# Layer 1's row maxima over whole rows, columns scaled ahead, and layer 3's V parts side by side

## The chip, the cores and the metric

The kernel runs on one core of one Trainium2 chip. The metric is the device time of one execution in microseconds. Its matrix engine is called TensorE (PE in the profile, PEld for its weight loads), and besides it there are VectorE (DVE), ScalarE (ACT), GpSimd (POOL), and SyncE (SP), which here only issues DMAs.

## The reference, cut to what matters

Eight graphs of 1024 nodes with 128 features go through four attention layers that share one adjacency matrix. Each layer's output is added to its input and normalised. Layer 0 and 1 are dot product attention with four heads of 32, layer 2 is additive with one head of 128, layer 3 additive with four heads of 32:

```python
# layer 1
scores = jnp.einsum('bhnd,bhmd->bhnm', q, k) / jnp.sqrt(jnp.float32(HD))
scores = jnp.where(adj[None, None] == 0, -jnp.inf, scores)
attn = jnp.nan_to_num(jax.nn.softmax(scores, axis=-1), nan=0.0)
# layers 2 and 3
e = ei[:, :, :, None] + ej[:, :, None, :]
e = jnp.where(e > 0, e, ALPHA * e)
e = jnp.where(adj[None, None] > 0, e, MASK_VAL)
att = jax.nn.softmax(e, axis=-1)
h = jnp.einsum('bhij,bhjd->bhid', att, Wh)
```

## The kernel before, in words

The program is a row of stages: `node(0)`, `heads(0)`, `node(1)`, `heads(1)` and so on to `node(4)`. A node stage goes over the eight graphs, makes the projections and stores them in DRAM. A heads stage runs one attention layer over its *units*, a unit being one head of one graph: 32 units in layers 0, 1 and 3, eight in layer 2. Four units make the body of a loop (`UNROLL`).

A unit has 16 *tiles* of 128 keys by 512 queries, eight for the first half of the queries and eight for the second. TensorE makes the scores of a tile in a PSUM bank, ScalarE takes the exponential, which is kept in a high part `phi` and, made by a subtraction (`take_low`, line 334), a low part `plo`; GpSimd makes the low part, VectorE every fourth in layer 1. Six tiles later (`LAGS`) TensorE weighs V with both parts (`weigh`). V is in three bf16 parts of 33 columns (32 and a column of ones for the sum): the high part of the weight meets all three, the low part two. In layer 1 a product takes the three parts side by side, 99 and 66 columns (lines 1095, 1097), into three results that VectorE adds. In layer 3 there are five products of 33 columns (line 1113), all into one result, and three more for rows without neighbours (line 1120).

PSUM has eight banks. In layers 1 to 3 the scores go round four of them (`RING`), banks 4 and 5 hold scores for the maxima, 6 and 7 the sums. The softmax needs each row's maximum, the *shift*, before the unit's first tile. In layer 1 `top_scores` multiplies 128 queries by 512 keys, with the maximum taken by `take_max` (line 1399) over each half row, 16 of them a unit, in a rhythm of one for each tile, one and a half units ahead. `find_shift` joins the halves (line 1362), `turn_shift` has TensorE transpose the result (line 1033), `shift_rows` copies it from PSUM (line 1377), and SP writes it in one transfer into row 96 of `qs` (`place_shift`, line 534). In layers 2 and 3 `spread` fills banks 4 and 5 with one row for all partitions (line 1010), `take_max` takes eight maxima of 1024 columns (line 1389), and `find_shift` makes the shift (lines 1367, 1368) and three scaled columns `colx` (1369 to 1371). The shift is placed by eight transfers of 128 elements (line 530). `settle` (line 1432) and a relu on ScalarE (line 839) prepare the argument of the exponential in layers 2 and 3. Lines 1070 and 1072 are the products of scores there, 1056 and 1057 in layer 1.

Each maximum waits for the one before:

```python
dve.wait_ge(s_nmax, CREDIT + TILES * U + k)
it, c = k // 2, k % 2
dve.wait_ge(s_nsc, TILES * U + k + 1)
```

At the end of each half unit `half_done` (lines 1479 to 1486) divides the sums by the last column and puts them in `outp`. SP's queue runs in this order in a unit: store the previous unit, place the next unit's shift, load the unit three ahead. Line 1325 copies the columns of a graph in stages 2 and 3 out of PSUM; `turn_x` on TensorE (line 935) waits for it. Line 1458 is layer 0's reduction over eight key blocks. In layer 1 a unit's loads are needed when its first `top_scores` comes up.

Of the kernel before, what the change touches and what calls it, by code (L numbers as in the profile page):

```python
# [34 lines left out]
P = 128  # L35
# [23 lines left out]
SHIFT_CREDIT = 1  # L59
# [5 lines left out]
MAX_AT = 8  # L65
TURN_AT = 11
TURN_BANK = 5

SPREAD_AT = 7
MAX_NEXT = {1: 6, 2: 7}  # L70
FIND_AT = 4
MAX_AFTER = {7: 0, 9: 1, 11: 2, 13: 3, 14: 4, 15: 5}
# [6 lines left out]
LOADS = (9, 7, 7, 8)  # L79
ROWMS = (0, 1, 8, 8)  # L80

SKEW = (0, 2, 2, 2, 1)
HCHAIN = (36, 32, 52, 28)
HLEFT = (7, 4, 6, 3)
# [6 lines left out]
def build(nc, t):  # L91
    with ExitStack() as ctx:
# [18 lines left out]
        col_d = nc.dram_tensor("col_d", (GRAPHS * 8, P, BLOCKS), F32, kind="Internal").ap()  # L111
# [46 lines left out]
        colp = sb("colp", [P, 8, BLOCKS])  # L158
# [17 lines left out]
        cols = sb("cols", [P, UNROLL, 2, BLOCKS])  # L176
        colx = sb("colx", [P, UNROLL, 3, BLOCKS])
# [11 lines left out]
        junk = full[:, 1, :].bitcast(BF16)[:, 0:NODES]  # L189
# [4 lines left out]
        shrow = sb("shrow", [BLOCKS, 2, P], F32R)  # L194
# [3 lines left out]
        sums = work[:, 0:2, :].rearrange("p t f -> p (t f)")[:, 0:IB * 33].rearrange("p (t d) -> p t d", d=33)  # L198
# [26 lines left out]
        s_colx = sem("s_colx")  # L225
# [14 lines left out]
        s_shT = sem("s_shT")  # L240
        s_shift = sem("s_shift")
# [108 lines left out]
        def max_count(U):  # L350

            return CREDIT + TILES * SHIFT0[2] + BLOCKS * (U - SHIFT0[2])
# [36 lines left out]
        def _(sp):  # L389
# [31 lines left out]
            def node(stage):  # L421
# [17 lines left out]
                def store_parts(b):  # L439
# [7 lines left out]
                    else:  # L447
                        n = 2 * HEADS[stage]
                        sp.wait_ge(s_ev["row2"], ev("row2", stage, b))
                        for kind in range(4):  # L450
# [3 lines left out]
                        sp.dma_start(col_d[bass.ds(b * 8, n)].rearrange("r p t -> p r t"), colp[:, 0:n, :]  # L454
                                     ).then_inc(s_pst[q], 16)
# [35 lines left out]
            def load_unit(layer, u, m):  # L491
# [16 lines left out]
                else:  # L508
# [7 lines left out]
                    for k in range(2):  # L516
                        go(cols[:, n, k, :], one(col_d, r + k * heads).rearrange("a p t -> (a p) t"))
# [7 lines left out]
            def place_shift(layer, g, n):  # L525
                if layer > 1:

                    sp.wait_ge(s_shcol, SHIFT0[layer] + g + 1)
                    for it in range(BLOCKS):
                        sp.dma_start(qs[96:97, n, it * P:(it + 1) * P].bitcast(F32), nshift[:, n % 2, it:it + 1]  # L530
                                     ).then_inc(s_rowm[n], 16)
                    return
                sp.wait_ge(s_shift, SHIFT_CREDIT + SHIFT0[layer] + g + 1)
# [54 lines left out]
        def _(pool):  # L588
# [110 lines left out]
            node(0)  # L699
            heads(0)  # L700

            pool.memset(ks[96:97, :, :].bitcast(F32), 1.0).then_inc(s_krow, 1)
            pool.wait_ge(s_krow, 1)
            node(1)
            heads(1)
# [903 lines left out]
```

## Time and profile before

| what | value |
|---|---|
| median of 3 runs | 3119.71 us (3115.49 to 3122.32) |
| profiled execution | 3143.97 us, its span 3142.2 us |
| busy, share of span | PE 77%, PEld 53%, DVE 70%, ACT 50%, POOL 58% |
| layer 0, about | 150 to 760 us |
| layer 1, about | 950 to 1685 us |
| layer 2, about | 1885 to 2205 us |
| layer 3, about | 2370 to 3065 us |
| mean granted clock of TensorE | 0.837 |

The rest of the span is node stages. Times in the trace count from the start of the span. A row of the timeline gives start and duration of one instruction, and in brackets how long its engine had been idle and what released it. A busy time is the time in which an engine had an instruction at work; a TensorE instruction in the trace lasts longer than its share, since matmuls overlap, so distances between starts say more.

### The profile page before, as it was taken

Reading aid. Unit: us, or ns where it says so; the run is one execution under the profiler, and the core shown is the slowest. Engines: PE = TensorE matmul, PEld = TensorE weight load, DVE = VectorE, ACT = ScalarE, POOL = GpSimd, SP = SyncE. Lnnn points to the kernel's source line nnn. Section 1 sums busy time; section 2 is a strip of 40 time slices with the busy share of each in tenths; the row PEclk is TensorE's granted clock in tenths of the full one; section 3 lists DMA queues with packets and bytes.
Section 4 is the critical chain, followed back from the end, with each engine's and each line's share of the span. In section 5 each row is a group of like instructions: output and inputs, shape, how many; then the busy total and the mean of one; then the engine's idle time right before and its main releaser. Section 6 shows DMA issues by size and latency. Waiting matters only on the chain.

```text
span 3142.2 us, 90847 instructions
## 1 busy us (share of the span) xinstructions
PE 2413.1 (77%) x33112; PEld 1668.6 (53%) x33112; DVE 2194.8 (70%) x4654; ACT 1585.7 (50%) x2273; POOL 1829.2 (58%) x1837
## 2 busy tenths in 40 slices
PE   5588888885657888888885758888466999999990
PEld 3366666664533555555554535667343666666660
DVE  4499999997656777777774335443456988888874
ACT  2344444453652444444443533444463777777775
POOL 2388888886433555555564433344323877777782
PEclk8788888887777999999997767889676988888995
DMA  7922222232653121212113641110452111111117
GB/s 236 300 73 74 73 73 73 73 74 47 192 206 85 49 54 45 56 45 52 48 46 80 185 146 42 49 32 15 132 133 56 49 48 49 39 47 49 44 25 162
DMA packets 299864, 263.65 MB, mean 84 GB/s; under 512 B 193080, under 2 KB 257080, under 8 KB 299504
## 3 DMA queue, kind: packets, MB, share of 16 engines
q1 hardware_dynamic: 294896, 241.82, 28.4%
q0 software_dynamic: 4608, 16.78, 1.5%
q8 instruction: 257, 4.21, 0.6%
q14 instruction: 103, 0.84, 0.1%
HBM read 162.84 MB, written 95.36 MB: 82 GB/s over the span
## 4 chain that ended last, share of the span: by engine, by line
PE 38%; issue 22%; DVE 22%; ACT 7%; POOL 3%; DMA 2%; DVEq 1%; SPq 1%; ACTq 0%; POOLq 0%
PE ps L1113 13%; PE ps L1072 4%; DVE xn L1458 4%; DVE full L1399 4%; PE ps L1010 3%; DVE full L1389 2%; PE ps L948 2%; PE ps L1053 2%; ACT xn L728 2%; PE ps L1065 2%; DVE cv L1420 2%; PE ps L1070 2%; POOL xc L334 2%; PE ps L1024 2%; PE ps L972 2%
## 5 line engine op out<-in xcount | busy, mean ns | idle before, releaser
L334 POOL TENSOR_TENSOR xc<-part 128x512 f16<-128x512 f32 x1536 | 1579.6, 1054 | 824.2 <-ACT part L865 672.5
L1113 PE MATMUL ps<-vs,part 128*128 128x33 bf16 (+1 forms) x13824 | 854.2, 189 | 45.8 <-DVEq L1490 44.5
L1113 PEld LDWEIGHTS ps<-vs,part 128*128 128x128 bf16 x13824 | 680.0, 101 | 362.3 <-issue 206.6
L1113 PE MATMUL ps<-vs,xc 128*128 128x33 bf16 (+1 forms) x9216 | 781.0, 187 | 3.8 <-issue 3.8
L1113 PEld LDWEIGHTS ps<-vs,xc 128*128 128x128 f16 x9216 | 597.5, 99 | 0.0
L865 ACT ACTIVATE part<-ps 128x512 f32<-128x512 f32 x512 | 305.8, 597 | 434.3 <-PE ps L1057 434.1
L1399 DVE CUSTOM_DVE_ANT_0 full<-ps,mask_n 128x512 bf16<-128x512 f32 x512 | 353.0, 690 | 161.9 <-DVE top L1399 61.0
L1389 DVE CUSTOM_DVE_ANT_0 full<-ps,mask_n 128x1024 bf16<-128x1024 f32 x320 | 390.4, 1220 | 108.0 <-PE ps L1010 79.4
L847 ACT ACTIVATE part<-cv,lift 128x1024 f32<-128x1024 f32 x256 | 294.8, 1152 | 322.0 <-DVE cv L1420 297.0
L1072 PE MATMUL ps<-qs,sel 128*128 128x512 f32 x640 | 420.1, 658 | 0.0
L1053 PE MATMUL ps<-qs,ks 128*128 128x512 f32 x512 | 290.6, 570 | 120.3 <-DVE cv L1420 88.2
L1432 DVE SCALAR_TENSOR_TENSOR cv<-ks,colx,ps 128x512 f32<-128x512 f32 x320 | 238.7, 746 | 186.5 <-PE ps L1072 145.9
L865 ACT ACTIVATE part<-cv,cols 128x512 f32<-128x512 f32 x320 | 229.9, 718 | 265.3 <-DVE cv L1432 249.4
L1024 PE MATMUL ps<-ks,qs 96*128 96x512 f32 x512 | 253.6, 506 | 116.6 <-DVE top L1399 94.2
L1420 DVE SCALAR_TENSOR_TENSOR cv<-ps,mask_t 128x1024 f32<-128x1024 f32 x256 | 311.8, 1219 | 44.5 <-PE ps L1053 22.0
L1057 PE MATMUL ps<-qs,ks 97*128 97x512 f32 x512 | 307.1, 600 | 0.0
L865 ACT ACTIVATE part<-ps,colx 128x512 f32<-128x512 f32 x320 | 215.1, 672 | 69.6 <-PE ps L1072 65.4
L1095 PE MATMUL ps<-vs,part 128*128 128x99 bf16 x2048 | 232.7, 213 | 1.8 <-POOL xc L334 1.8
L1095 PEld LDWEIGHTS ps<-vs,part 128*128 128x128 bf16 x2048 | 164.2, 99 | 129.8 <-issue 103.9
L839 ACT ACTIVATE ps<-ks,colx 128x512 f32<-128x512 f32 x316 | 218.7, 692 | 11.5
L1097 PE MATMUL ps<-vs,xc 128*128 128x66 bf16 x2048 | 219.3, 195 | 0.0
L1056 PE MATMUL ps<-mask_t,ident_b 128*128 128x512 bf16 x512 | 205.0, 400 | 0.4
(151 smaller groups left out, 3607.5 us busy)
## 6 DMA issues: line engine op xcount, KB each, us to landing
qs<-q_d SPq DMA_DIRECT2D x224, 128.0 KB
ks<-k_d SPq DMA_DIRECT2D x224, 128.0 KB
ks<-row_d SPq DMA_DIRECT2D x40, 512.0 KB
vs<-v_d SPq DMA_DIRECT2D x96, 198.0 KB
q_d<-part SPq DMA_DIRECT2D x32, 512.0 KB
k_d<-part SPq DMA_DIRECT2D x32, 512.0 KB
ctx_d<-xn SPq DMA_DIRECT2D x96, 128.0 KB, 1.7
xc<-ctx_d SPq DMA_DIRECT2D x96, 128.0 KB, 4.6
```

What stands on the lines that cost most here:

```text
L334: eng.tensor_tensor(plo[:, r, :], prob[:, r, :], phi[:, r, :], ALU.subtract).then_inc(low_done(layer, u, s)[0], 1)
L847: act.activation(prob[:, r:r + 2, :], arg[:, a:a + 2, :], ACT.Exp, scale=2.0 * CLIP, bias=lift[:, 0:1]).then_inc(s_exp, 2)
L865: act.activation(prob[:, r, :], src, ACT.Exp, **more).then_inc(s_exp, 1)
L1024: pe.matmul(bank, qs[0:96, n, it * P:(it + 1) * P], ks[0:96, n, cut], start=True, stop=True).then_inc(s_nsc, 1)
L1053: mm = pe.matmul(bank, ks[:, n, blk_j], qs[:, n, cut], start=True, stop=True)
L1057: mm = pe.matmul(bank, ks[0:97, n, blk_j], qs[0:97, n, cut], start=False, stop=True)
L1072: mm = pe.matmul(bank, sel[:, 2, :], qs[:, n, cut], start=False, stop=True, skip_group_check=True)
L1095: pe.matmul(ps[:, 6 + c, at_a:at_a + V3], phi[:, r, it * P:(it + 1) * P], vs[:, n, at_v:at_v + V3], start=opens, stop=False, skip_group_ch ...
L1113: mm = pe.matmul(acc, half[:, r, it * P:(it + 1) * P], vs[:, n, at:at + width], start=opens and h == 0 and v == 0, stop=h == 1 and v == 1, ...
L1389: dve.tensor_tensor_reduce(junk[:, :], pf[:, 4 * HALF:6 * HALF], mask_n[:, k, :], 1.0, LOWEST, ALU.add, ALU.max, accum_out=top[:, k, 0:1]) ...
L1399: dve.tensor_tensor_reduce(junk[:, 0:HALF], ps[:, 4 + c, :], mask_n[:, it, c * HALF:(c + 1) * HALF], 1.0, LOWEST, ALU.add, ALU.max, accum_ ...
L1420: dve.scalar_tensor_tensor(arg[:, a:a + 2, :], ps[:, r:r + 2, :], -0.5, mask_t[:, j:j + 2, c * HALF:(c + 1) * HALF], ALU.max, ALU.min).the ...
```

## The change

**Layer 1's maxima.** `top_scores` makes two products into a pair of banks, (2, 3) or (4, 5) in turn, and `take_max` takes the maximum of the whole row of 1024 straight into `nshift`: eight a unit. A maximum waits for the last but one. The scores' ring in layer 1 becomes two banks, 0 and 1. `turn_shift`, `shift_rows` and layer 1's `find_shift` go; the shift is placed by eight transfers as in layers 2 and 3, and row 96 of `ks` holds -1 where it held 1. The maxima of the unit after next come at tiles 5, 7, 9, 11, 13 and 15, the last two at tiles 1 and 3 of the next.

**Scaled columns.** `colx` goes. The node stages 2 and 3 make five columns for each head (two copies, three scalings), one DMA loads them.

**Layer 3.** The products are layer 1's (99 and 66 columns), and the correction is one product of 99. `half_done` in layers 1 and 3 takes the divisor from the first part, scales all three parts into `sums` (384 elements), and a reduction adds them into `outp`.

In all three layers the maxima write their unused output to two buffers in turn (`junks`).

```diff
-MAX_AT = 8
-TURN_AT = 11
-TURN_BANK = 5
+MAX_NEXT = ({}, {1: 6, 3: 7}, {1: 6, 2: 7}, {1: 6, 2: 7})
+MAX_AFTER = ({}, {5: 0, 7: 1, 9: 2, 11: 3, 13: 4, 15: 5}) + ({7: 0, 9: 1, 11: 2, 13: 3, 14: 4, 15: 5},) * 2
...
-LOADS = (9, 7, 7, 8)
-ROWMS = (0, 1, 8, 8)
+LOADS = (9, 7, 6, 7)
+ROWMS = (0, 8, 8, 8)
...
-        junk = full[:, 1, :].bitcast(BF16)[:, 0:NODES]
+        junks = [full[:, k, :].bitcast(BF16)[:, 0:NODES] for k in range(2)]
...
-                    for k in range(2):
-                        go(cols[:, n, k, :], one(col_d, r + k * heads).rearrange("a p t -> (a p) t"))
+                    go(cols[:, n, :, :], one(col_d, g).rearrange("a p k t -> (a p) k t"))
...
+                if layer == 1:
+                    sp.wait_ge(s_nmax, max_count(g + 1))
+                else:
+                    sp.wait_ge(s_shcol, SHIFT0[layer] - SHIFT0[2] + g + 1)
+                for it in range(BLOCKS):
+                    sp.dma_start(qs[96:97, n, it * P:(it + 1) * P].bitcast(F32), nshift[:, n % 2, it:it + 1]
+                                 ).then_inc(s_rowm[n], 16)
...
@@ top_scores
+                    at = 2 + 2 * (k % 2)
+                    pe.wait_ge(s_nmax, max_count(U) + k - 1)
+                    for c in range(2):
+                        mm = pe.matmul(ps[:, at + c, :], qs[0:96, n, k * P:(k + 1) * P],
+                                       ks[0:96, n, c * HALF:(c + 1) * HALF], start=True, stop=True)
+                    mm.then_inc(s_nsc, 1)
...
-                            bank = ps[:, s % RING, :]
+                            bank = ps[:, s % (2 if layer else RING), :]
...
-                                pe.wait_ge(s_exp, T - RING + 1)
+                                pe.wait_ge(s_exp, T - 2 + 1)
...
-                            if layer == 1:
+                            if layer in (1, 3):
...
+                                if layer == 3 and j == BLOCKS - 1:
+                                    at_i = c * HALF + it * P
+                                    mm = pe.matmul(ps[:, 6 + c, at_a:at_a + V3], empty[:, at_i:at_i + P], zs[:, n, :],
+                                                   start=False, stop=True, skip_group_check=True)
...
-                        dve.tensor_copy(colp[:, 0:n, :], ps[:, 4, 0:BLOCKS * n].rearrange("p (t r) -> p r t", r=n)
-                                        ).then_inc(s_ev["col"], 1)
+                        for k in range(2):
+                            dve.tensor_copy(colp[:, 0:heads, k, :], got[:, :, k, :])
+                        dve.tensor_scalar(colp[:, 0:heads, 2, :], got[:, :, 1, :], SLOPE - 1.0, None, ALU.mult)
+                        dve.tensor_scalar(colp[:, 0:heads, 3, :], got[:, :, 1, :], 1.0 - SLOPE, None, ALU.mult)
+                        dve.tensor_scalar(colp[:, 0:heads, 4, :], got[:, :, 1, :], SLOPE, None, ALU.mult
+                                          ).then_inc(s_ev["col"], 1)
...
@@ take_max
+                    dve.wait_ge(s_nmax, max_count(U) + k - 1)
+                    if layer == 1:
+                        src, least, dst = pf[:, (2 + 2 * (k % 2)) * HALF:][:, 0:NODES], LEAST, nshift[:, n % 2, k:k + 1]
+                        dve.wait_ge(s_nsc, BLOCKS * U + k + 1)
...
+                    dve.tensor_tensor_reduce(junks[k % 2], src, mask_n[:, k, :], 1.0, least, ALU.add, ALU.max,
+                                             accum_out=dst).then_inc(s_nmax, 1)
...
@@ half_done
-                            if layer == 1:
-                                acc = sums
-                                link(dve.tensor_reduce(acc, ps[:, bank, 0:IB * V3].rearrange(
-                                    "p (t v d) -> p t d v", v=3, d=33), AX.X, ALU.add))
...
+                            link(dve.tensor_scalar(rden[:, 0:blocks], acc[:, :, 0, width], TINY, None, ALU.max))
                             link(dve.reciprocal(rden[:, 0:blocks], rden[:, 0:blocks]))
...
+                            link(dve.tensor_tensor(sums, acc[:, :, :, 0:width],
+                                                   scale.unsqueeze(3).to_broadcast([P, blocks, parts, width]), ALU.mult))
+                            link(dve.tensor_reduce(o, sums.rearrange("p t v d -> p t d v"), AX.X, ALU.add))
```


## Rows read from the trace of the kernel before

**Rows 1.** Windows, three attention layers: us, each engine's busy us, granted clock, DMA share.

```profile
1000.00:1640.00 640.00, 545.22 (x5021) 331.41 (x5020) 481.32 (x1303) 271.14 (x454) 366.97 (x341) 0.97 0.20 50
1960.00:2160.00 200.00, 169.09 (x1787) 132.37 (x1785) 90.30 (x201) 84.77 (x122) 82.43 (x81) 0.85 0.12 35
2440.00:3040.00 600.00, 563.50 (x10953) 383.95 (x10951) 521.87 (x1002) 450.33 (x691) 465.35 (x461) 0.90 0.18 44
```

**Rows 2.** Waits in layer 1, 1000 to 1640: total us, times, longest.

```profile
PE ps L1024 <- DVE top L1399: 90.7, 107, 2.4
DVE full L1399 <- DVE top L1399: 52.3, 196, 0.3
```

**Rows 3.** Groups by line, VectorE in layer 1: busy us, mean ns, idle before.

```profile
L1399 DVE CUSTOM_DVE_ANT_0 full<-ps,mask_n 128x512 bf16<-128x512 f32 x453 | 312.3, 689 | 133.5 <-DVE top L1399 52.3 <-PE ps L1024 34.4 <-DVE xn L1486 30.5
L334 DVE TENSOR_TENSOR xc<-part 128x512 f16<-128x512 f32 x113 | 85.2, 754 | 4.9 <-PE ps L1097 4.4 <-DVE nshift L1362 0.4
...
L1479 DVE TENSOR_REDUCE work<-ps 128x132 f32<-128x396 f32 x57 | 32.2, 566 | 0.0
```

**Rows 4.** Layer 1's shift by line: ns min/median/max, first and last start.

```profile
L1362 DVE SCALAR_TENSOR_TENSOR nshift<-top x32: 166/167/462, 969.0 to 1661.7; 128x8 f32<-128x8 f32 x32
```

**Rows 5.** Timeline, TensorE's score products near layer 1's end: start, us.

```profile
1655.51 0.59 PE L1057 MATMUL ps<-qs,ks 97*128 97x512 f32 x1
...
1656.61 0.59 PE L1057 MATMUL ps<-qs,ks 97*128 97x512 f32 x1
...
1659.57 0.59 PE L1057 MATMUL ps<-qs,ks 97*128 97x512 f32 x1
...
1660.35 0.58 PE L1057 MATMUL ps<-qs,ks 97*128 97x512 f32 x1
```

**Rows 6.** Layer 3's shift by line, 2440 to 3040.

```profile
L1368 DVE SCALAR_TENSOR_TENSOR nshift<-shift x29: 166/966/966, 2446.2 to 3031.7; 128x8 f32<-128x8 f32 x29
```

**Rows 7.** Timeline, VectorE in layer 3: end of a half, maxima, a settle.

```profile
2603.97 0.16 DVE L1483 TENSOR_SCALAR rden<-ps 128x4 f32<-128x4 f32 x1
...
2604.38 0.29 DVE L1486 TENSOR_TENSOR xn<-ps,rden 128x128 f32<-128x128 f32 x1
2605.05 1.22 DVE L1389 CUSTOM_DVE_ANT_0 full<-ps,mask_n 128x1024 bf16<-128x1024 f32 x1 [0.38 <-DVE xn L1486]
...
2606.20 0.74 DVE L1432 SCALAR_TENSOR_TENSOR cv<-ks,colx,ps 128x512 f32<-128x512 f32 x1
2606.86 1.22 DVE L1389 CUSTOM_DVE_ANT_0 full<-ps,mask_n 128x1024 bf16<-128x1024 f32 x1
```

**Rows 8.** Timeline, TensorE's score products in layer 3.

```profile
2471.33 0.58 PE L1072 MATMUL ps<-qs,sel 128*128 128x512 f32 x1
...
2472.30 0.58 PE L1072 MATMUL ps<-qs,sel 128*128 128x512 f32 x1
```

**Rows 9.** Layer 0's reduction in SBUF by line.

```profile
L1458 DVE TENSOR_REDUCE xn<-work x64: 1898/1998/2025, 161.1 to 746.9; 128x128 f32<-128x1024 f32 x64
```

**Rows 10.** Timeline, opening of layer 3: SP's small transfers and their release.

```profile
2387.01 22.65 SPq L530 DMA_DIRECT2D qs<-nshift  x16
...
2393.53 0.58 PE L1070 MATMUL ps<-mask_t,ident_b 128*128 128x512 bf16 x1 [2.09 <-DMA qs<-nshift]
```

**Rows 11.** Timeline, TensorE at a turn of layer 3's loop.

```profile
2647.51 0.60 PE L1070 MATMUL ps<-mask_t,ident_b 128*128 128x512 bf16 x1 [3.69 <-issue]
```

**Rows 12.** Windows behind a turn of layer 1's loop.

```profile
1150.00:1158.00 8.00, 5.85 (x34) 3.50 (x34) 4.08 (x12) 1.55 (x4) 2.08 (x2) 0.57 0.00 1
1158.00:1162.00 4.00, 4.00 (x39) 2.35 (x38) 3.50 (x8) 2.25 (x4) 3.13 (x3) 1.00 0.00 0
```

**Rows 13.** Timeline, VectorE in layer 3: first scaled column, next settle.

```profile
2611.84 0.15 DVE L1369 SCALAR_TENSOR_TENSOR colx<-cols 128x8 f32<-128x8 f32 x1
...
2613.13 0.75 DVE L1432 SCALAR_TENSOR_TENSOR cv<-ks,colx,ps 128x512 f32<-128x512 f32 x1
```

**Rows 14.** The copy of the columns: who waited for it (us, times).

```profile
  PE ps L935: 40.7, 14
```

More of the change, by code:

```diff
@@ L525, in place_shift @@
             def place_shift(layer, g, n):
[L526 to L533, printed above, removed]
-                sp.dma_start(qs[96:97, n, :].bitcast(F32).rearrange("a (t p) -> a t p", p=P),
-                             shrow[:, n % 2, :].bitcast(F32)).then_inc(s_rowm[n], 16)
+                if layer == 1:
[5 more added lines that the diff above has]
+                                 ).then_inc(s_rowm[n], 16)
             def store_output(layer, g, n):
@@ L852, in exps @@
                         if layer == 1:
-                            src, more = ps[:, r % RING, :], dict(scale=SCALE)
+                            src, more = ps[:, s % 2, :], dict(scale=SCALE)
                             act.wait_ge(s_score, T - CREDIT + 1)
@@ L1115, in weigh @@
                                                    skip_group_check=True)
-                            if layer == 3 and j == BLOCKS - 1:
-                                at_i = c * HALF + it * P
-                                for v in range(3):
-                                    mm = pe.matmul(acc, empty[:, at_i:at_i + P], zs[:, n, v * 33:(v + 1) * 33],
-                                                   start=False, stop=v == 2, skip_group_check=True)
                         mm.then_inc(s_av, 1)
@@ L1150, in heads @@
+                            if tt in MAX_AFTER[1] and one_after:
+                                if MAX_AFTER[1][tt] == 0:
+                                    unit_ready((n + 2) % UNROLL, u + (n + 2) // UNROLL)
+                                top_scores((n + 2) % UNROLL, MAX_AFTER[1][tt], U + 2)
                 if layer:
                     U = SHIFT0[layer]
-                    if layer == 1:
-                        unit_ready(0, 0)
-                        for k in range(TILES):
-                            top_scores(0, k, U)
-                        turn_shift(0, U)
-                    else:
-                        for n in range(2):
-                            unit_ready(n, 0)
-                            spread(n, U + n)
@@ L1162, in heads @@
-                    if layer == 1:
-                        unit_ready(1, 0)
-                        pe.wait_ge(s_shift, SHIFT_CREDIT + U + 1)
-                        for k in range(TILES - MAX_AT):
-                            top_scores(1, k, U + 1)
+                    for n in range(2):
+                        unit_ready(n, 0)
+                        if layer > 1:
+                            spread(n, U + n)
+                            continue
+                        for k in range(BLOCKS if n == 0 else len(MAX_AFTER[1])):
+                            top_scores(n, k, U + n)
@@ L1229, in _ @@
             dve.memset(bias3[:, :, :], 0.0).then_inc(s_fill, 1)
-            left, cut = work[:, 0:4, :], junk[:, 0:HALF].rearrange("p (k f) -> p k f", f=F)
+            left, cut = work[:, 0:4, :], junks[1][:, 0:HALF].rearrange("p (k f) -> p k f", f=F)
             given = rows[:, 0:4, :]
@@ L1405, in body @@
+                    if k == BLOCKS - 1 and layer > 1:
+                        dve.wait_ge(s_nmax, max_count(U + 1))
                 def body(u, first, last):
```

161 lines of the change are left out of this document (47 added, 114 removed).

## The prediction

> **What bounds the kernel now.** I read the windows of the three attention layers that change [rows 1]. No engine is full in layer 1: TensorE has work in 545 of 640 us, VectorE in 481. So I asked the waits who is late [rows 2]: TensorE stands 90.7 us at the score products for the maxima, behind VectorE's previous maximum, and VectorE itself stands 52.3 us behind its own accumulator. The groups of VectorE [rows 3] give the size: a maximum over 512 columns takes 0.69 us and has 0.29 us of idle time before it, 0.98 us in all, 16 times a unit, 15.7 us. The shift is found once a unit, 32 times from 969.0 to 1661.7 [rows 4]: 692.7 us over 31 periods, 22.35 us a unit. TensorE's own need is read where it is not held up [rows 5]: successive score products are 1.10 us apart with one product for a maximum in between (1655.51 to 1656.61) and 0.78 us without (1659.57 to 1660.35). Sixteen tiles need 17.6 us. So layer 1 goes at VectorE's pace and has 4.75 us a unit to lose.
>
> Layer 3 is another case. Its period is (3031.7 - 2446.2) / 28 = 20.91 us [rows 6]. VectorE works in 521.9 of 600 us [rows 1]; its slots are tight [rows 7]: a maximum over 1024 columns 1.15 us from start to start, a settle 0.66 us, one after the other, eight of each 14.5 us. TensorE's tiles are 0.97 us apart [rows 8], 15.5 us for sixteen, and two one-row products come on top. Both engines are close to the bound. Layer 2 has VectorE at 90 of 200 us: what the change does there on VectorE lies in its idle time.
>
> **Layer 1, step by step.** The maxima become eight of 1024 columns. They no longer wait for their predecessor (two junk buffers), so each is 1.15 to 1.22 us: 9.5 us instead of 15.7. Four subtractions at 0.75 us stay [rows 3], 3.0 us. The end of a half unit changes: in layer 3 it now lasts 1.08 us, 2603.97 to 2605.05, with a product of 128 elements of 0.29 us [rows 7]. After the change the product covers 384 elements: the 396 elements of the old layer 1 reduction took 0.57 us [rows 3], so 0.55, +0.26. Behind it comes a new reduction of 384 elements in SBUF. Bounds: 0.57 us by the reduction from PSUM; from above by layer 0's reduction, 1024 elements, 1.998 us [rows 9], which also jumps between the terms of each sum: less a fixed 0.15 it is 1.8 ns an element, so 0.84 us. I take the upper, the nearer in memory and pattern; with a gap the half grows by 1.15 us to 2.25, two of them 4.5 us. VectorE then needs 9.5 + 3.0 + 4.5 = 17.0 us, TensorE still 17.6 (same products, one transpose less): TensorE becomes the bound, by little. The transpose and VectorE's copy of its result go and free VectorE.
>
> *The shift's way.* It was one transfer after tile 11. Now eight small ones wait for the eighth maximum (tile 3), but on SP's queue they stand behind the store of the previous unit, which waits for the end of its half, about tile 6. I reckon: tiles 0 to 5 of the unit 6.0 us (six at 0.78 and four products for maxima at 0.32), tile 5's own two products to 6.7, their maximum to 7.9, the end of the half to 10.0, the store 0.5 (an allowance), then eight transfers. In the opening of layer 3 they take from 2387.01 to the release at 2393.53, 6.5 us [rows 10]. That lands at 17.0 us, and the next unit starts at 17.6. So it is hidden by 0.6 us alone; if VectorE runs late by more, all of it shows. The seven loads stand behind these issues and end early enough for the maxima of two units on (needed at tile 5 of the next unit), again with little over. I put 0.3 us on the unit: 17.9.
>
> *The scores' ring* falls from four banks to two. A bank must be read before it is written again: scores, then the exponential. Two tiles last 1.56 us even without products for maxima, 2.2 us with. The exponential runs beside them. I cost it at nothing; without its cover it is a rival below.
>
> *The turn of the loop.* TensorE stands still for 3.69 us at the start of a body [rows 11], and the clock then falls: in 1150 to 1158 the granted clock is 0.57, so mostly the lower level of 1.2 GHz, and 34 matmuls start, where the next 4 us at 1.00 (2.4 GHz) start 39 [rows 12]. Eight microseconds did the work of 3.5, 4.5 lost with an idle of 2.15; with an idle of 3.7 it is 6.1, per unit 1.5. While VectorE set the pace this was partly hidden; with TensorE as bound it counts: 17.9 + 1.5 = 19.4, rounded to 19.5. **Layer 1: 31 x (22.35 - 19.5) = 88 us less.** Bounds: 17.9 (no turn cost) is 138 less; 20.6 (VectorE late by 1.1 us) is 54 less. The opening has 16 maxima at about 0.95 before any score, then 8 at 1.2: 5 us less.
>
> **Layer 3.** Twenty matmuls of 33 columns in each tile become eight of 99 and 66. The nearest rows are the tiles themselves: 0.97 us here, 0.78 us in layer 1 with just such a tile [rows 5, 8], so TensorE gets 16 x 0.19 = 3.0 us a unit, and 16 of 24 correction products. VectorE loses 2 x 1.15 = 2.3 us at the halves. It wins the three scaled columns: from 2611.84 to the settle at 2613.13, 1.29 us [rows 13], of which 0.2 comes back as a wait: 1.1. Adjacent maxima win 0.2. Its idle time is 78 us in some 29 units, 2.7 us each; I let TensorE's relief take 0.5 of it. Net +0.5 us a unit, **16 us more**. Bounds: a reduction of 0.57 and 1.0 us of waits gone, -0.5 a unit, 16 less; nothing gone, +1.0, 32 more.
>
> **The rest.** In stages 2 and 3 one copy of the columns becomes five small operations, and TensorE waits for this copy, 40.7 us over 14 times [rows 14]. A small operation takes 166 ns at least [rows 6], and these overlap since none waits for another; I take 0.1 us for each of the four added, bounds 0 and 0.166: 16 x 0.4 = 6 us more, at most 11. The column loads are one DMA fewer a unit, hidden in SP's idle time; stored pieces are longer. The openings of layers 2 and 3 lose some 14 waits behind an accumulator, 4 us less. Layer 2's steady part: 0.
>
> **Sum:** -88 - 5 + 16 + 6 - 4 = -75. The profiled execution took 3143.97 us, span 3142.2, 0.8% over the median of 3119.71. 3144 - 75 = 3069; on the median 3045 us.
>
> **Rivals.**
> *A, more is won:* layer 1 runs at TensorE's 17.6 with the turn cheaper, or layer 3, freed of TensorE, gains: 120 to 150 us less, 2985. For it: cold stretches also hit layer 3's TensorE, clock 0.90 [rows 1]. Against: VectorE's tight slots [rows 7].
> *B, less is won:* the shift's 0.6 us of cover is gone, or VectorE sets 20.6 us: 54 and 5 won, 32 and 6 lost, 4 won: 25 less, 3095.
> *C, slower:* the new reduction in SBUF waits for GpSimd. A small operation on SBUF there, nshift, is 166 ns when GpSimd is idle and 966 at the median beside it [rows 6]. If reduction and product each wait 0.8 us, 3.2 us a unit in both layers: VectorE needs 20.2 in layer 1, with the turn 21.7, a gain of 20; layer 3 loses 32 x 3.7 = 118. With the rest that is 95 more, 3215. It is slower from about 1.6 us a unit on (75 = 31 x (1.6 - 0.9) + 32 x 1.6). Against: layer 0's reduction spans 1898 to 2025 ns with GpSimd busy [rows 9], no such scatter. The Trainium skill (GPSIMD Engine Reference, the row on SBUF interfaces in section 1) names DVE instructions with two SBUF inputs or in a 2-port mode as those that contend; the product has one SBUF input, the reduction one, nshift two, which agrees with the spread above.
> *D, the clock:* with two banks TensorE idles briefly and often and drops to 1.2 GHz. Layer 1 before had 90.7 us of such stops at 0.97 [rows 1, 2], so against. If a quarter of layer 1 were cold, its unit would be 17.6 x 1.25 = 22, with the turn 23.5: 36 more there, and 13 for the rest: 3170. The Trainium skill warns of it (TensorE: Matmul & The Clock Gate, "A second HAM failure mode: psum-queue depth-cycling"): cycling through PSUM banks makes the clock oscillate. No row here shows it without a longer stop.
>
> **Numbers.** Forecast case (3015 to 3075) 0.47, A 0.22, B 0.18, C 0.07, D or no gain at all 0.06. Two in ten left out: 2985 to 3095. This kernel's measurement tells 0.2% (6 us). Faster 0.87, same 0.03, slower 0.10.
>
> **What the new profile would show.** Layer 1: TensorE's waits for maxima gone, period near 19.5, VectorE's reduction at 0.84 us, the release of tile 0 by the DMA of nshift rare. Layer 3: period 21.4, VectorE over 0.9 busy, TensorE's tiles with gaps, and its clock no lower. Wrong if tile 0 waits for nshift each unit, if the reduction is over 1.2 us, or if layer 1's clock falls below 0.9.

## The result, and the profile after

The changed kernel takes 2980.9 us (median of 4 executions, 2975.7 to 2990.5) where the kernel before takes 3121.0: a ratio of 0.955, 95% interval 0.952 to 0.958. The forecast was 3045 us, the range 2985 to 3095. The direction was right, the gain of 140 us almost twice the 75 forecast. The profiled execution is the longest of the four, 2990.5 us, its span 2988.8.

The windows of the changed kernel, as [rows 1] (layers 1, 2 and 3):

```profile
1000.00:1500.00 500.00, 487.81 (x4984) 302.40 (x5076) 462.42 (x806) 275.59 (x463) 397.77 (x346) 1.00 0.28 64
1800.00:2000.00 200.00, 167.38 (x1899) 135.33 (x1929) 90.83 (x192) 90.54 (x130) 88.07 (x86) 0.91 0.12 35
2260.00:2860.00 600.00, 504.28 (x4611) 300.08 (x4692) 514.55 (x933) 425.38 (x658) 440.07 (x439) 0.84 0.16 42
```

TensorE is busy 98% in layer 1 (85% before) at full clock, while layer 3's clock fell from 0.90 to 0.84. The waits in layer 1, as [rows 2]:

```profile
DVE full L1344 <- DVE xn L1436: 28.3, 57, 0.6
...
PE ps L1034 <- DMA qs<-nshift: 7.9, 17, 1.6
PE ps L1034 <- issue: 2.2, 3, 1.0
DVE full L1344 <- PE ps L1009: 1.9, 4, 0.9
```

TensorE's 90.7 us behind maxima are gone and nothing of that size came instead; the shift's transfers cost 7.9 us in 500. They were not rare, as forecast: tile 0 waited for them 17 times in some 29 units. VectorE's groups there, as [rows 3]:

```profile
L1344 DVE CUSTOM_DVE_ANT_0 full<-ps,mask_n 128x1024 bf16<-128x1024 f32 x229 | 274.7, 1215 | 31.2 <-DVE xn L1436 28.3 <-PE ps L1009 1.9 <-issue 1.0
L328 DVE TENSOR_TENSOR xc<-part 128x512 f16<-128x512 f32 x116 | 123.1, 1061 | 0.3 <-DVE xn L1436 0.3
L1436 DVE TENSOR_REDUCE xn<-work 128x128 f32<-128x384 f32 x58 | 34.6, 596 | 2.0
L1434 DVE TENSOR_TENSOR work<-ps,rden 128x384 f32<-128x384 f32 x58 | 32.3, 557 | 2.0
```

The new reduction takes 0.60 us, the low part rose from 0.75 to 1.06. A layer's length is read here from its first to its last exponential. First the kernel before, then the changed one (duration, first and last start; the first row is layer 1, the second spans layers 2 and 3):

```profile
L865 ACT ACTIVATE part<-ps x512: 597/597/603, 978.0 to 1678.0; 128x512 f32<-128x512 f32 x171
L865 ACT ACTIVATE part<-cv,cols x320: 705/722/728, 1900.4 to 3058.3; 128x512 f32<-128x512 f32 x160
```

```profile
L855 ACT ACTIVATE part<-ps x512: 591/597/599, 970.6 to 1522.1; 128x512 f32<-128x512 f32 x171
L855 ACT ACTIVATE part<-cv,cols x320: 704/721/727, 1740.9 to 2902.4; 128x512 f32<-128x512 f32 x160
```

Read so for every run (us from the first to the last exponential of a layer, one profiled execution each; "median" is of the whole kernel):

| kernel | layer 1 | layer 2 | layer 3 | median, executions |
|---|---|---|---|---|
| before | 700.0 | 304.2 | 659.2 | 3121.0, 4 |
| before, once more (`y1`) | 699.7 | 283.3 | 658.8 | 3123.1, 1 |
| changed | 551.5 | 284.2 | 683.8 | 2980.9, 4 |
| `x1` parts in PSUM | 550.8 | 283.6 | 668.6 | 2972.4, 4 |
| `x2` columns by VectorE | 551.1 | 284.2 | 681.5 | 2996.7, 4 |
| `x3` one junk buffer | 553.9 | 283.9 | 666.3 | 2988.1, 4 |
| `x5` layer 1's part alone | 548.5 | 304.0 | 668.5 | 2985.8, 4 |
| `x4` before, short maxima | 635.8 | 283.7 | 658.6 | 3055.5, 1 |
| `y2` more instructions | 593.0 | 284.3 | 658.7 | 3007.5, 1 |
| `y4` more low parts | 602.1 | 284.3 | 680.4 | 3031.2, 1 |
| `z1`, `z2`, `z4` padded | 554.9, 551.8, 552.6 | 294.0, 304.1, 283.5 | 670.9, 708.8, 679.4 | 2989.5, 3030.8, 2977.5, 1 each |
| `z3` before, padded | 698.4 | 283.9 | 658.5 | 3115.5, 1 |
| `x7` spread early | 551.8 | 284.0 | 750.1 | 3051.5, 4 |
| `x8` spread early, parts in PSUM | 550.9 | 283.8 | 680.9 | 2982.9, 4 |
| `x9` spread early, layer 1's part alone | 550.8 | 284.8 | 681.8 | 2990.7, 1 |
| `y3` filler | 552.2 | 284.3 | 651.3 | 2952.4, 4 |
| `z5` filler, layer 2's spread early | 552.4 | 283.7 | 657.9 | 2958.4, 4 |
| `z6` half filler | 552.0 | 283.6 | 661.1 | 2966.1, 4 |

The ledger from `y1` (3123.1 us) to the changed kernel's profiled execution (2990.5): the start of layer 1 -7.6, layer 1 -148.2, the stage behind it with layer 2's opening -5.0, layer 2 +0.9, the next stage -0.5, layer 3 +25.0, the rest +2.8. Sum -132.6.

### The profile page after: what moved, and what is told of

Its sections match the earlier page's. It is cut to its first block, busy times and chain, and to the rows that moved or that the text cites. A ratio compares the mean times of both kernels' runs of the same rounds, so it can differ in the third digit from the quotient of the medians.

```text
span 2988.8 us, 75947 instructions
## 1 busy us (share of the span) xinstructions
PE 2279.6 (76%) x26182; PEld 1544.6 (52%) x26424; DVE 2185.2 (73%) x4086; ACT 1581.0 (53%) x2273; POOL 1846.1 (62%) x1837
## 4 chain that ended last, share of the span: by engine, by line
PE 37%; DVE 22%; issue 19%; ACT 7%; SPq 5%; DMA 4%; POOL 2%; DVEq 1%; ACTq 0%; POOLq 0%
PE ps L1092 8%; PE ps L1050 4%; DVE xn L1402 4%; DVE full L1344 4%; PE ps L1000 3%; SPq L526 3%; PE ps L1073 3%; PE ps L1031 3%; PE ps L938 2%; DVE cv L1364 2%; DVE cv L1376 2%; ACT xn L720 2%; PE ps L1009 2%; PE ps L1075 2%; PE ps L1035 2%
## 5 line engine op out<-in xcount | busy, mean ns | idle before, releaser
L1344 DVE CUSTOM_DVE_ANT_0 full<-ps,mask_n 128x1024 bf16<-128x1024 f32 x576 | 695.2, 1218 | 173.8 <-PE ps L1000 106.2
L1092 PE MATMUL ps<-vs,part 128*128 128x33 bf16 (+1 forms) x7680 | 504.5, 193 | 45.8 <-DVEq L1437 44.5
L1073 PE MATMUL ps<-vs,part 128*128 128x99 bf16 x4096 | 496.4, 218 | 2.8 <-POOL xc L328 2.8
L1075 PE MATMUL ps<-vs,xc 128*128 128x66 bf16 x4096 | 468.9, 200 | 0.0
L1092 PE MATMUL ps<-vs,xc 128*128 128x33 bf16 (+1 forms) x5120 | 458.7, 191 | 3.5 <-issue 3.5
L1050 PE MATMUL ps<-qs,sel 128*128 128x512 f32 x640 | 424.2, 664 | 26.7 <-DVE cv L1376 21.2
L1075 PEld LDWEIGHTS ps<-vs,xc 128*128 128x128 f16 x4096 | 360.9, 103 | 0.0
L1376 DVE SCALAR_TENSOR_TENSOR cv<-ks,cols,ps 128x512 f32<-128x512 f32 x320 | 238.4, 745 | 156.5 <-PE ps L1050 130.0
L1364 DVE SCALAR_TENSOR_TENSOR cv<-ps,mask_t 128x1024 f32<-128x1024 f32 x256 | 311.8, 1219 | 42.9 <-PE ps L1031 19.3
L1092 PEld LDWEIGHTS ps<-vs,xc 128*128 128x128 f16 x5120 | 342.0, 100 | 0.0
L855 ACT ACTIVATE part<-ps,cols 128x512 f32<-128x512 f32 x320 | 214.8, 671 | 74.3 <-PE ps L1050 69.4
L829 ACT ACTIVATE ps<-ks,cols 128x512 f32<-128x512 f32 x316 | 218.6, 692 | 11.1
L1031 PEld LDWEIGHTS ps<-qs,ks 128*128 128x128 f32 x512 | 110.7, 217 | 131.8 <-DVE cv L1364 90.3
```

The source lines that it names most:

```text
L855: act.activation(prob[:, r, :], src, ACT.Exp, **more).then_inc(s_exp, 1)
L1031: mm = pe.matmul(bank, ks[:, n, blk_j], qs[:, n, cut], start=True, stop=True)
L1050: mm = pe.matmul(bank, sel[:, 2, :], qs[:, n, cut], start=False, stop=True, skip_group_check=True)
L1073: pe.matmul(ps[:, 6 + c, at_a:at_a + V3], phi[:, r, it * P:(it + 1) * P], vs[:, n, at_v:at_v + V3], start=opens, stop=False, skip_group_ch ...
L1075: mm = pe.matmul(ps[:, 6 + c, at_a:at_a + 66], plo[:, r, it * P:(it + 1) * P], vs[:, n, at_v:at_v + 66], start=False, stop=True, skip_grou ...
L1092: mm = pe.matmul(acc, half[:, r, it * P:(it + 1) * P], vs[:, n, at:at + width], start=opens and h == 0 and v == 0, stop=h == 1 and v == 1, ...
```

## Experiments

A loop's *turn* is its jump back to its start. In layers 1 and 3 the loop has five turns: four units make a body, and the first units and the last ones are made outside it. An *undisturbed* unit is one that is neither at a turn nor at low clock. Units are read from one store of a unit's output to the next.

**Undoing the parts one at a time.** Four kernels. `x1` gives layer 3 its 20 products of 33 columns a tile and the short end of a half back:

```diff
-                            if layer in (1, 3):
+                            if layer == 1:
...
-                            parts = 1 if layer == 2 else 3
+                            parts = 3 if layer == 1 else 1
```

> The changed kernel with layer 3's three parts of V summed in PSUM again, as before the change (20 products of 33 columns a tile, end of a half with one product of 128 elements). Changed kernel: 2980.9 us. Theory 1 (VectorE sets layer 3's pace, its two longer halves are what costs): VectorE gets 2 x 0.9 us a unit back, the undisturbed units go from 20.2 to 18.5 or so and the whole to 2925 to 2950. Theory 2 (the loss of layer 3 is only the stretches of low clock, and TensorE's relief pays for VectorE's longer halves): undisturbed units stay at 20.1 to 20.4, the whole at 2970 to 2985 with the same or fewer cold stretches. If the form of before is worse, 2995.

Measured: 2972.4 us, ratio to before 0.954 (0.951 to 0.958), an interval that overlaps the changed kernel's. Layer 3 takes 668.6, its undisturbed units 20.1 to 20.2 us, so neither VectorE's 2 us a unit nor theory 1's 18.5 showed. Its waits in layer 3 (2300 to 2860), and those of the changed kernel, say why:

```profile
PE ps L1048 <- issue: 22.1, 5, 4.9
```

```profile
DVE cv L1376 <- issue: 10.3, 5, 2.2
```

With 20 products a tile TensorE is the bound (busy 515 of 560 us) and stands 4.4 us at each turn of the loop, waiting for nothing. With eight it does not, and VectorE (477 of 560) stands 2.1 us instead. The two units around a turn exceed two undisturbed ones by 5 to 8 us with 20 products and by about 2.4 with eight.

`x2` lets VectorE make the three scaled columns in `find_shift` again, `x3` takes one junk buffer and makes each maximum wait for its predecessor:

```diff
+                    dve.scalar_tensor_tensor(colx[:, n, 0, :], col, SLOPE, col, ALU.mult, ALU.subtract)
+                    dve.scalar_tensor_tensor(colx[:, n, 1, :], col, -SLOPE, col, ALU.mult, ALU.add)
+                    dve.scalar_tensor_tensor(colx[:, n, 2, :], col, SLOPE - 1.0, col, ALU.mult, ALU.add
+                                             ).then_inc(s_colx, 1)
```

```diff
-                    dve.wait_ge(s_nmax, max_count(U) + k - 1)
+                    dve.wait_ge(s_nmax, max_count(U) + k)
...
-                    dve.tensor_tensor_reduce(junks[k % 2], src, mask_n[:, k, :], 1.0, least, ALU.add, ALU.max,
+                    dve.tensor_tensor_reduce(junks[1], src, mask_n[:, k, :], 1.0, least, ALU.add, ALU.max,
```

> The changed kernel with the three scaled columns of layers 2 and 3 made by VectorE in every unit again (three small operations and the wait behind them; the nodes still store five columns). Theory 1 (these columns are layer 2's 20 us: they stand between two settles and TensorE waits for them): layer 2 takes 15 to 20 us more, layer 3 another 20 to 30, the whole 3015 to 3030. Theory 2 (layer 2's gain came from the clock or from the junk buffers, the columns cost only their own 1.1 us a unit in layer 3): layer 2 within 5 us, layer 3 +30 at most, the whole 2985 to 3010.

> The changed kernel with one junk buffer and each maximum waiting for the one before it, in layers 1 to 3. Theory 1 (layer 1 is bound by TensorE with room on VectorE, layers 2 and 3 have adjacent maxima in three places only): layer 1 plus 0 to 10, layers 2 and 3 plus 0.2 us a unit, 8 us, openings plus 5: 2985 to 3000. Theory 2 (layer 2's 20 us are the junk buffers' and layer 1 lives from them): 3005 to 3040, with layer 2 near 304 us and waits of TensorE for maxima in layer 1.

`x2`: 2996.7 us, 0.961 (0.958 to 0.964), so 16 slower. Layer 3's undisturbed units are 21.2 us instead of 20.3, 0.9 us for the columns where the prediction took 1.1; layer 2 keeps 284. `x3`: 2988.1, 0.959 (0.956 to 0.963); 7 slower, 2.4 of it in layer 1. Neither accounts for layer 2's 20 us.

`x5` has both of these and `x1`'s edit in layers 2 and 3, and layer 1 as changed:

> Layer 1's part of the change alone in the layers (whole-row maxima, two junk buffers, two banks for the scores, shift without the transpose); layers 2 and 3 work as before the change (parts summed in PSUM, scaled columns by VectorE, one junk buffer). Theory 1 (each layer's time is its own): layer 1 about 552 us, layer 2 about 304, layer 3 about 659, so 3121 - 148 - 7 - 3 = 2963, range 2955 to 2972. Theory 2 (layer 2's and 3's times follow from how warm TensorE's clock comes into them or from code that is shorter): layer 2 at 284 also here, whole 2940 to 2950.

Measured: 2985.8 us, 0.956 (0.954 to 0.959). Layer 1 548.5, and layer 2 at 304 again. All that the change did to layers 2 and 3 together is worth 5 us, inside the scatter of the executions. Layer 3 came out at 668.5, 9 above the 659 forecast.

**Layer 1's turn.** In the kernel before, VectorE's first maximum behind the turn waits for nothing for 2.9 us, and TensorE for it (timeline: start, duration, and in brackets the idle time):

```profile
1151.40 0.69 DVE L1399 CUSTOM_DVE_ANT_0 full<-ps,mask_n 128x512 bf16<-128x512 f32 x1 [2.92 <-issue]
...
1152.15 0.79 PE L1024 MATMUL ps<-ks,qs 96*128 96x512 f32 x1 [2.33 <-DVE top L1399]
```

So layer 1's stop is VectorE's. `x4` takes VectorE work away without an instruction less; it takes the maxima over half their columns:

```diff
-                    dve.tensor_tensor_reduce(junk[:, 0:HALF], ps[:, 4 + c, :], mask_n[:, it, c * HALF:(c + 1) * HALF],
+                    dve.tensor_tensor_reduce(junk[:, 0:HALF // 2], ps[:, 4 + c, 0:HALF // 2],
+                                             mask_n[:, it, c * HALF:c * HALF + HALF // 2],
```

> The kernel before, with each of layer 1's sixteen maxima of a unit taken over 256 columns instead of 512: it leaves out half of the maxima's work, the number of instructions stays. VectorE has some 4.3 us a unit less to do and falls below TensorE's need. Theory 1 (the turn of the loop costs only where VectorE is the bound; it is VectorE's own stop that TensorE waits for): units near 17.6 and no longer ones at the turns, layer 1 from first to last exponential 550 to 560 us instead of 700. Theory 2 (the turn's cost comes with the number of instructions in the body): every fourth unit 4 to 5 us longer, as before, layer 1 585 to 600.

Neither number was met: units of 19.5 us, every fourth 24 to 25.7, layer 1 635.8. The waits in layer 1, 1000 to 1500:

```profile
DVE full L1399 <- PE ps L1024: 80.2, 112, 1.6
PE ps L1024 <- DVE top L1399: 41.6, 53, 2.7
DVE full L1399 <- DVE top L1399: 28.2, 104, 0.3
...
DVE full L1399 <- issue: 16.3, 5, 3.6
```

VectorE now waits for TensorE 80 us and TensorE for VectorE 42: product and maximum of half a row alternate, and 4.3 us less work gave 2.1 us a unit (64 us over 31). The stop at the turn stayed, 3.3 us each time. The reverse, on the changed kernel: `y2` adds instructions without work, `y4` work with fewer added instructions.

```diff
-                    dve.sem_inc(s_carry, 1)
+                    for _ in range(6 if layer == 1 else 1):
+                        dve.sem_inc(s_carry, 1)
```

```diff
-DVE_LOW = ((), (3,), (), ())
+DVE_LOW = ((), (1, 3), (), ())
```

> The changed kernel with five more semaphore increments ahead of each of layer 1's maxima on VectorE, 40 a unit, about as many instructions as the eight maxima that the change took away. Theory 1 (VectorE's stop at the turn of the loop comes with the number of instructions in its body and went with them): stops of 2 to 3 us that wait for nothing are back in layer 1 at the turns, every fourth unit 2 to 4 us longer; the layer 15 to 30 us longer. Theory 2 (the stop went because longer instructions cover it): no stop; units longer by what 40 increments take, 0 to 2 us, all alike.

> The changed kernel with every second low part of layer 1 made by VectorE instead of every fourth (four more subtractions of 1.06 us a unit), so that VectorE, now busy 94%, becomes layer 1's bound. Theory 1 (the turn's cost shows only when VectorE is the bound): units of 20.3 to 20.6 and every fourth 2 to 4 us longer. Theory 2 (it went with the instructions): units of 20.3 to 20.6, all alike; the whole near 3075 either way.

`y2`: layer 1 593.0, 41.5 longer where 15 to 30 was expected. Behind the first units the one at a turn takes 20.3 to 20.6, the one behind it 19.3 to 20.5, the others 17.3 and 19.0. `y4`: 602.1, units of 18.7 and every fourth 20.2; less than the 20.3 expected, as the low part takes 0.79 us on the mean of 500 us and not 1.06, and less than 2 to 4 us more at a turn. Behind the turn, on the timelines of `y2` and `y4`:

```profile
1123.33 0.69 DVE L328 TENSOR_TENSOR xc<-part 128x512 f16<-128x512 f32 x1 [3.04 <-ACT part L855]
```

```profile
1123.74 0.69 DVE L328 TENSOR_TENSOR xc<-part 128x512 f16<-128x512 f32 x1 [2.32 <-PE ps L1075]
```

These come once in a body, 3.0 and 2.3 us; in `y2` the last exponential of the body before had ended at 1116.68, long before VectorE fell idle at 1120.29, so I read them as the stop, under the name of an old release. It is back in both, five times in each. It does not need a VectorE that is the bound: VectorE is busy 423 of 500 us in `y2` (1000 to 1500), less than the 462 of the changed kernel, which has no stop, and 325 in `x4`, which has it.

Counted in the traces from one branch to the next, waits and register instructions included, VectorE's body in layer 1 has 466 instructions in the kernel before and in `x4`, 290 in the changed kernel, 450 in `y2` and 338 in `y4`. So `y4` too has 48 more, and all the bodies from 338 up stop at the turn, the one of 290 does not. Behind the last pass, where the loop is left, none stops.

Whether the place of the code matters was told by padding that is run once, ahead of the first layer, with N of 32, 96 and 160, and 64 in the kernel before:

```diff
             node(0)
+            for _ in range(N):
+                dve.sem_inc(s_carry, 1)
             heads(0)
```

> The changed kernel with 32 semaphore increments more in VectorE's program, once, ahead of the first attention layer: no loop gets longer, all loops of VectorE lie further on in its program. Theory 1 (VectorE's stop at the turn of a loop depends on where the loop's code lies): in at least one of the three padded versions the stops change place: layer 1's units of 17.3 get a longer fourth one, or layer 3's fourth units fall from 22.7 to 20.6. Theory 2 (it depends on the loop's own instructions alone): layer 1 17.3 throughout, layer 3 with 22.7 at every turn, VectorE with 5 stops of about 2.1 us in layer 3, in all three.

> As the version with 32 increments more, with 96. The same two theories and numbers.

> As the version with 32 increments more, with 160. The same two theories and numbers.

> The kernel before with 64 semaphore increments more in VectorE's program, once, ahead of the first attention layer. Theory 1 (place of the code): VectorE's stops of 3.0 us at layer 1's turns get shorter or go, every fourth unit falls from 26.8 towards 22, the layer from 680 to 645 to 670 us between its first and last store. Theory 2 (the loop's own instructions): 26.8 at every turn and 680 us, as in both executions of the kernel before.

In layer 1 theory 2 holds: 17.3 us a unit with no longer fourth one in all three, and every fourth unit at 27.1 to 27.3 in the padded kernel before, its stops 2.6 us instead of 2.9. In layer 3 theory 1 holds: with 96 VectorE's five stops are gone, with 32 and 160 they are there (9.8 and 9.7 us). They are gone in `y2` and `y4` as well, whose longer layer 1 moves layer 3's code of the same 318 instructions. But `z2` is the slowest of the three, which leads to the clock.

**Layer 2: 284 or 304.**

> The kernel before, unchanged, in one more profiled execution. Its shown profile took 3144.0 us, where the median of the unprofiled executions is 3121. Theory 1 (layer 2's units of 40.9 us are a matter of the execution, as the same operations took 37.6 in the kernel with short maxima in layer 1): units of 37.6 here, layer 2 near 284 us, the whole 3115 to 3125. Theory 2 (the change shortened layer 2 by work): 40.9 again.

The same kernel gave 283.3 in its second execution. From layer 2 of the shown profile of before (one unit), then of the changed kernel, the windows between TensorE's stops, columns as in [rows 1]:

```profile
1986.50:1997.50 11.00, 11.00 (x67) 7.28 (x66) 2.73 (x4) 2.09 (x3) 1.06 (x2) 0.53 0.51 144
1997.50:2010.50 13.00, 9.37 (x126) 7.68 (x124) 7.88 (x18) 6.32 (x10) 7.20 (x7) 1.00 0.06 25
2010.50:2014.50 4.00, 4.00 (x37) 3.48 (x34) 0.83 (x2) 1.38 (x2) 1.04 (x1) 0.57 0.00 0
2014.50:2027.50 13.00, 10.45 (x139) 8.50 (x138) 7.16 (x19) 7.03 (x10) 7.16 (x7) 1.00 0.00 1
```

```profile
1820.00:1824.00 4.00, 3.86 (x24) 2.97 (x25) 0.03 (x1) 0.62 (x1) 0.32 (x1) 0.57 0.41 132
1824.00:1840.00 16.00, 12.85 (x156) 9.89 (x156) 9.84 (x20) 7.79 (x12) 8.19 (x8) 1.00 0.27 86
```

Behind one of its two stops TensorE goes at the lower level of 1.2 GHz for some 10 us in the first and 4 us in the second; six microseconds more at half speed are about the 3.3 us between units of 40.9 and 37.6. In the long pattern the spread lies in the low clock, on the two timelines:

```profile
2029.87 3.78 PE L1010 MATMUL ps<-qs,sel 1*128 1x512 f32 x4
```

```profile
1860.91 2.07 PE L1000 MATMUL ps<-qs,sel 1*128 1x512 f32 x4
```

Both patterns repeat unit for unit. The changed kernel falls into the long one too (`z1` in part, `z2`). What selects it was not found. The gain of 20 us in the two shown profiles is not work saved by the change; whether the change makes the long pattern rarer is not shown.

**The spread's place.** `SPREAD_AT = 5` makes it ahead of the stop instead of behind (`x7`; `x8` with `x1`'s edit, `x9` with `x5`'s):

> The changed kernel with the one-row products of layers 2 and 3 (the spread) made after tile 5 of a unit, ahead of TensorE's stop for the end of a half at tile 6, instead of after tile 7, behind it. Theory 1 (a spread that falls into the low clock takes 3.8 us instead of 2.1, is itself part of what stretches the low clock, and VectorE waits for it, 35.2 us in 560): layer 2 stays at 37.6 us a unit or gets 1 shorter, the units of 23.7 to 26.0 in layer 3 get rare, undisturbed ones go from 20.3 to about 19.3; the whole 2930 to 2955 against 2980.9. Theory 2 (the wait only moves: TensorE then stands at the spread for VectorE's eighth maximum): within 0.3% of the changed kernel, or slower by up to 20 us.

> The changed kernel with layer 3's parts summed in PSUM again and the spread after tile 5. Layer 3 is then bound by TensorE (busy 515 of 560 us in the run with the parts in PSUM, 2972.4 us). Theory 1: VectorE's waits for the spread (22.2 us) are off the bound, the gain is only what the low clock gives back, some 10 us: 2955 to 2970, and slower than the changed kernel with the same spread. Theory 2 (VectorE's work still decides): 2930 to 2945, faster than it.

> Layer 1's part alone (layers 2 and 3 work as before the change), with the spread after tile 5. Layer 2 took 40.9 us a unit in that kernel and before the change, with low clock for 4 and 10 us in turn, where it took 37.6 in the three kernels that kept the new columns or the two junk buffers, with 4 us each time. Theory 1 (layer 2's gain is not work saved, but whether the spread falls into the low clock behind the stop): 37.6 or less here too, with the work of before the change. Theory 2 (the columns and the junk buffers save the time): 40 to 41 here.

Layer 2 did not gain (284.0, 283.8, 284.8; its first unit is longer by what the others save). Layer 3 was a surprise: in `x7` nearly all units take 22.6 to 24.1 us and those at turns 26, 750 in all and 3051.5 us, 0.977 (0.971 to 0.983); with 20 products a tile, `x8`, most take 20.3 to 20.6 and those at turns 27 to 28, at 2982.9, 0.956 (0.950 to 0.961). What makes nearly all of `x7`'s units slow is open. My theory that the early spread frees layer 3 is refuted.

**Work for TensorE.** The slow units of layer 3 remain: in the changed kernel nine of 23.6 to 26.0 us, in two rows of four and five, at a granted clock of mostly 0.66 to 0.76 over 20 us where the others have 0.91. One begins so (timeline, VectorE, then TensorE):

```profile
2385.45 0.75 DVE L1376 SCALAR_TENSOR_TENSOR cv<-ks,cols,ps 128x512 f32<-128x512 f32 x1 [2.10 <-issue]
...
2386.29 0.58 PE L1050 MATMUL ps<-qs,sel 128*128 128x512 f32 x1 [3.65 <-DVE cv L1376]
...
2392.56 3.78 PE L1000 MATMUL ps<-qs,sel 1*128 1x512 f32 x4
```

VectorE's stop at the turn holds TensorE for 3.65 us, the clock falls to 0.50, the spread takes 3.78 us, and VectorE waits for it, 37.0 us in 600. But such a unit needs no stop at a turn. `z2`, whose VectorE has none in layer 3, has the most slow units of the padded kernels, 20 of 23.6 to 24.0 us. TensorE's longest idle time there is 1.6 us. The wait that it belongs to (2260 to 2860), and the window of a slow unit:

```profile
PE ps L1048 <- DVE cv L1376: 30.2, 20, 1.6
```

```profile
2363.00:2387.00 24.00, 21.20 (x171) 12.43 (x173) 18.91 (x34) 15.59 (x24) 16.12 (x17) 0.71 0.16 41
```

`y4` has 11 of them and `y2` five, also without a stop. What the slow ones go with is the lighter products: no profile with 20 products a tile has one in layer 3 (the kernel before, `y1`, `x4`, `z3`, `x1`, `x5`, `x8`, `x9`), and with eight and no filler only `x2`'s has none, its fastest execution, with VectorE's units at 21.2. `y3` gives TensorE one product by zeros in each tile of layer 3:

```diff
+                            if layer == 3:
+                                pe.matmul(bank, none_b[:, :], mask_t[:, j, cut], start=False, stop=False,
+                                          skip_group_check=True)
```

> The changed kernel with one more product of 512 columns by zeros in each tile of layer 3 (16 a unit, 0.22 us each), which changes no result. Theory 1 (layer 3's loss is units of 23.7 to 26 us at low clock, since TensorE has too little to do; VectorE is the bound of the others): these units are gone, all are 20.2 to 20.5 but the turns at 22.7; layer 3 near 645 instead of 684 in the profiled run, the whole 2960 to 2972. Theory 2 (the low clock comes from the stop of 3.7 us at the turn alone, whatever else TensorE does): as many slow units, and each longer by up to 2 us: 2990 to 3020.

Measured: 2952.4 us (2949.6 to 2955.7), 0.945 (0.941 to 0.950), 28 below the changed kernel and some 8 below the range expected. Window and waits in its layer 3:

```profile
2260.00:2860.00 600.00, 543.66 (x5489) 319.23 (x5488) 534.75 (x971) 451.73 (x700) 468.44 (x467) 0.98 0.17 43
```

```profile
DVE cv L1381 <- issue: 10.0, 5, 2.1
...
DVE full L1349 <- PE ps L1001: 3.4, 5, 0.9
```

The slow units are gone, though the stops at the turns are the same (units there 22.6 to 23.5): theory 1. The undisturbed units stay at 20.1 to 20.2 with the clock at 1.00, where they are 20.1 to 20.4 with 0.91, so TensorE's clock does not bound these; VectorE, busy 535 of 600 us, most likely does. Last, two variants:

> The version with one product by zeros more in each tile of layer 3 (2952.4 us), and layer 2's spread after tile 5 instead of 7; layer 3's spread stays after tile 7. Theory 1 (in layer 2 the spread ahead of the stop stays out of the low clock): layer 2 from first to last store 217.6 instead of 222.3 us, as in the three versions with that place, and never the units of 40.9; the whole 2944 to 2950. Theory 2 (the gain is given back in the stage behind it): 2950 to 2955.

> The same version with layer 3's product by zeros over 256 columns instead of 512. Theory 1 (what counts is how much TensorE works between its stops): fewer slow units than the changed kernel's ten, but some of 23.7 are back; the whole 2950 to 2970. Theory 2 (any product more in the gaps is enough, and the shorter one delays the scores less): no slow units, the whole 1 to 5 us under the full filler's, 2940 to 2948. Theory 3 (half is as good as none): 2970 to 2980.

`z5`: 2958.4, 0.948 (0.947 to 0.950), nothing won over `y3`: nearer to theory 2, though 3 us above its range. `z6`, which is `z5` with the half product: 2966.1, 0.951 (0.949 to 0.953). The time is theory 1's, but the units are not: none over 23.1, and undisturbed ones of 20.6 to 21.0. So no theory holds as stated. The half product too removes the slow units, and costs 8 us against the whole one; why the undisturbed units are longer is open. `y3` is the fastest kernel of this study.

## Why the prediction was wrong

*Layer 1, the turn of the loop.* This is the step that failed: "with TensorE as bound it counts", 1.5 us a unit. It charged 31 x 1.5 = 47 us, and the changed kernel pays nothing: 17.3 us a unit at the turns as elsewhere. Three things were wrong in it. The row behind it [rows 11] is TensorE's own stop in layer 3, where its body has some 3190 instructions, with 20 products a tile; in layer 1 it has some 1600, and only waited for VectorE's stop. The cost was not "partly hidden" before but paid in full: the units at the five turns take 25.8 to 27.6 us where the others take 21.5 to 22.0, 25 us in all. So it was already in the 22.35 us a unit that the forecast started from. And five turns at the forecast's own 6.1 us are 30 us, not 47. That VectorE's stop is gone and not hidden is in the changed kernel's waits: 1.0 us of "issue" in 500. `y2` brings it back with nothing but instructions in VectorE's loop, `y4` with instructions and work; padding ahead of the loop does not. So the change itself removed it, by taking 44 instructions out of a unit of VectorE's loop. From how many on a body stops (between 290 and 338 here), and by which mechanism, is open.

*Layer 1, the rest.* 17.6 us for TensorE was 17.3, and the 0.3 for the shift's way was about 0.3 (7.9 us in 500, within the 17.3). With the rounding to 19.5, some 0.7 us a unit too much. Against this the 22.35 us of the kernel before, read from shift to shift, was 0.4 too high: from store to store it is 680.6 us over 31, 21.95 a unit, and 531.2 over 31, 17.1, in the changed kernel. That VectorE falls just below TensorE was right (462 and 488 busy of 500), with two errors of opposite sign: the reduction 0.60 instead of 0.84 us, 0.5 less a unit, the low part 1.06 instead of 0.75, 1.2 more. Two banks for the scores cost nothing, as forecast.

*Layer 3.* +16 forecast, +25 measured in the profiled execution (the longest of the four), but for another reason. Undisturbed units are 0.2 us longer (0.5 forecast), and the five turns some 3 us cheaper (not forecast), which together is a gain: `y3` has 651 us against 659 before. Nine units at low clock, some 3.4 us each, turn it into a loss. "Its clock no lower" was wrong: it went from 0.90 to 0.84. Rival D had that mechanism, but in layer 1. The Trainium skill (TensorE: Matmul & The Clock Gate, "A second HAM failure mode: psum-queue depth-cycling") warns of brief idle times between groups of matmuls. Layer 1's two banks show none of it, 1.00 over 500 us; layer 3, where TensorE got the lighter products, does, and more products cured it.

*Layer 2* at 0 was right, against the appearance of the two shown profiles. *The nodes and openings:* layer 1's opening 5 forecast, 7.6 measured with 2.7 of an earlier start; the rest +2 forecast, -5.5 measured. TensorE's wait for the columns rose by 5.2 us to 45.9 as forecast, but the stages as a whole did not get longer.

*Rivals.* A (more won) came closest, with its turn that costs less; its other half, a gain in layer 3, came only with `y3`'s filler. C is refuted: 596 ns a reduction beside GpSimd, no added wait.

## What to carry to other kernels

Find whose stop it is at the turn of a loop before charging it: look for the engine whose rows say "issue", count how many turns there are, and ask whether the measured period holds the stop already. It can vanish with instructions taken from that engine's loop. Before crediting a change with a stage's gain, run the old kernel's profile a second time. Where TensorE is not the bound, look at its granted clock before and after making its work lighter: here that brought units of low clock, and a useless product in each tile won them back.

## What the runs showed of the hardware that I had not expected

Low clock comes in patterns that hold for many units: layer 2 at 283.3 or 304.2 us in the same kernel, layer 3 from 659 (`y2`) to 709 (`z2`) with the same instructions in its loop. Such stretches came with idle times of TensorE of at most 1.6 us (`z2`). VectorE stops at the turns of layer 1's loop for 1.7 to 3.6 us with bodies of 338, 450 and 466 instructions and not with 290. In layer 3, with 318, it depends on the place of its code (present with 0, 32 and 160 increments ahead, gone with 96), and in layer 1 it did not in the positions tried. TensorE stops on its own for 3.1 us and more at turns of bodies of some 2800 (layer 0) and 3200 instructions (layer 3 with 20 products), and not with some 1500 to 1650. The four one-row products take 2.07 us at the full clock and 3.78 at the low one.
